# A Mamba block with routed experts: the second expert product in f16 halves, steps placed anew, and B broadcast one state at a time

## The reference

```
s = s * exp(delta * A) + delta * B * u          # per token, channel and state
y = sum over states of C * s, + u * D
...
g = sigmoid(x @ gate_w.T); the top 4 of 16, divided by their sum -> combine
h = silu(x @ e_win) * (x @ e_vin) * combine     # per expert: 256 -> 128
routed = h @ e_wout                             # 128 -> 256, summed over experts
shared = silu(x @ ws_in) * (x @ vs_in) @ ws_out # 256 -> 256 -> 256
x = x + gate * (routed + shared)
```

## Time and profile before

| | us |
|---|---|
| median of 3 runs (lowest to highest) | 2981.22 (2980.82 to 2988.78) |
| the profiled execution | 2980.19 |
| its span in the profile | 2978.4 |
| mean granted TensorE clock | 0.922 |

### The profile page before, as it was taken

One profiled execution on the slowest core, in us unless ns is written; L12 is line 12 of the kernel. 1 busy time (PEld: TensorE's weight loads), 2 busy tenths in 40 slices (PEclk: granted clock), 3 DMA queues, 4 the chain that ended last, 5 costly groups with the idle time before them and its releaser, 6 DMA issues.

```text
span 2978.4 us, 52216 instructions
## 1 busy us (share of the span) xinstructions
PE 2431.5 (82%) x16084; PEld 1908.7 (64%) x16084; DVE 2277.2 (76%) x3495; ACT 2129.4 (71%) x4033; POOL 2397.0 (80%) x2382
## 2 busy tenths in 40 slices
PE   3557988888797888979888797888979788897879
PEld 1335767667576665757667575766757666676767
DVE  4777778787787878778787877878777787877753
ACT  4786877778686777868677787767868777785641
POOL 1887898889788888888888888888978878897842
PEclk7657999999899999999999899999989999998999
DMA  1775777867676785767677677776757777676841
GB/s 67 195 172 127 167 159 164 179 135 161 147 170 157 165 177 132 163 158 162 155 156 178 138 163 158 156 171 150 167 135 169 160 165 172 135 159 140 179 102 57
DMA packets 154563, 455.99 MB, mean 153 GB/s; under 512 B 22280, under 2 KB 24968, under 8 KB 154032
## 3 DMA queue, kind: packets, MB, share of 16 engines
q0 software_dynamic: 73728, 268.47, 48.2%
q1 hardware_dynamic: 80560, 184.20, 19.9%
HBM read 166.29 MB, written 17.87 MB: 62 GB/s over the span
## 4 chain that ended last, share of the span: by engine, by line
POOL 21%; issue 20%; PE 18%; DVE 15%; ACT 14%; DMA 6%; DVEq 1%; POOLq 0%; ACTq 0%; SPq 0%
POOL db_sb L669 10%; PE bank_ps L1413 8%; DVE states L1150 5%; PE moe_ps L1431 4%; POOL y_sb L681 3%; POOL act L712 3%; DMA y_sb<-c_rows 3%; DMA th_p<-x_dram 3%; ACT c_rows L886 3%; ACT da_ps L913 3%; PE rows_ps L1349 2%; DVE bank_ps L1097 2%; POOL y_sb L690 2%; DVE act L1231 2%; DVE act L1237 1%
## 5 line engine op out<-in xcount | busy, mean ns | idle before, releaser
L669 POOL TENSOR_TENSOR db_sb<-du_sb,b_sb 128x512 f32<-128x512 f32 x1024 | 1575.2, 1710 | 80.3 <-DVE states L1150 79.8
L886 ACT ACTIVATE c_rows<-rows_ps,xd_sb 128x512 f32<-128x512 f32 x1024 | 684.8, 684 | 186.4 <-PE rows_ps L1349 93.9
L1349 PE MATMUL rows_ps<-ident,states 128*128 128x128 f32 x4096 | 646.8, 291 | 177.6 <-ACT c_rows L886 104.9
L913 ACT ACTIVATE da_ps<-delta,a_sb 128x512 f32<-128x512 f32 x1024 | 704.4, 692 | 93.2 <-DVE states L1150 91.5
L712 POOL TENSOR_TENSOR act<-act,w_sb 128x256 f32<-128x256 f32 x512 | 580.8, 1185 | 224.7 <-DMA w_sb<-w_dram 119.4
L681 POOL DMA_DIRECT2D y_sb<-c_rows x512 | 608.2, 1195 | 149.9 <-DMA y_sb<-c_rows 77.1
L1431 PE MATMUL moe_ps<-eout_sb,act 128*128 128x256 f32 x2304 | 621.5, 395 | 103.8 <-POOL act L712 101.6
L1150 DVE TENSOR_TENSOR_SCAN states<-da_ps,carry,db_sb 128x512 f32<-128x512 f32 x512 | 649.3, 1276 | 54.1 <-ACT da_ps L913 52.3
L1349 PEld LDWEIGHTS rows_ps<-ident,states 128*128 128x128 f32 x4096 | 512.6, 150 | 273.8 <-DVE states L1150 123.6
L1413 PE MATMUL bank_ps<-h2T_high,ein_w_high 128*128 128x256 f16 x2304 | 643.2, 279 | 36.0 <-DVE h2T_low L1133 15.0
L1150 DVE TENSOR_TENSOR_SCAN states<-da_ps,db_sb 128x512 f32<-128x512 f32 x512 | 617.4, 1215 | 69.2 <-ACT da_ps L913 68.3
(11 more groups left out here) (169 smaller groups left out, 2633.8 us busy)
## 6 DMA issues: line engine op xcount, KB each, us to landing
y_sb<-c_rows POOLq DMA_DIRECT2D x512, 512.0 KB, 5.5
b_sb<-b_dram SPq DMA_DIRECT2D x128, 512.0 KB, 5.1
w_sb<-w_dram SPq DMA_DIRECT2D x256, 256.0 KB, 4.4
th_p<-x_dram SPq DMA_DIRECT2D x16, 512.0 KB, 8.2
r_dram<-conv SPq DMA_DIRECT2D x16, 512.0 KB, 2.8
x<-r_dram SPq DMA_DIRECT2D x16, 512.0 KB, 5.8
out_dram<-x SPq DMA_DIRECT2D x32, 256.0 KB, 2.3
mod_p<-mod_dram SPq DMA_DIRECT2D x7, 384.0 KB, 11.2
```

What stands on the lines that cost most here:

```text
L669: pool.tensor_tensor(db_sb[:, n % NDB, :], du_sb[:, slots[t][0][0], b, :], b_sb[:, k % NBPAIR, s % BPAIR, :], ALU.mult).then_inc(sem["scal ...
L886: ac.activation(c_rows[:, n % NCR, j % CPAIR, :], rows_ps[j % 2][:, :], ACT.Copy, scale=xd_sb[:, slots[t][0][0], j, s:s + 1]).then_inc(sem ...
L913: ac.activation(da_ps[n % NDA][:, :], delta[:, slots[t][0][0], b, :], ACT.Exp, scale=a_sb[:, b, s:s + 1]).then_inc(sem["exp_done"], 1)
L1349: last = pe.transpose(rows_ps[j % 2][:, b * P:b * P + P], states[:, step % 2 * NB + b, j * P:j * P + P], ident[:, :])
```

## The change

Two things change beside the tables.

*The second expert product in f16 halves.* `eout_sb` (f32) becomes `eout_w16`, a high and a low f16 tile of the weights, lifted by 64. They are made during slot 1 in nine steps: `eo_load` (SP) brings two experts' weights into the buffers of `w_sb`, `eo_high` (ACT) writes the high part and `eo_low` (DVE) the remainder. In a unit, `e_weigh` moves ahead of `e_mul` and now needs only `e_act`. `e_mul` waits for `e_weigh` and writes its product back into the right half of the bank. Two steps are new: `e_high` (ACT) copies that half to f16 and `e_low` (DVE) writes the difference, which frees the bank. `expert_out` is six f16 matmuls. The f16 tiles have two buffers, the ring `act` keeps three. The shared units are scaled inside `e_mul`, and POOL's one-time `eout_fold` goes.

*B one state at a time.* `BPAIR, NBPAIR` go from 2, 2 to 1, 4: 256 loads of 256 KB, each of which waits until `scaled` is done with the state four before it.

All the tables have new numbers. The router's scratch tiles now lie in `zg`, so the next slot's `z_tanh` also waits for the router of the last one, and `dt_low` waits for both copies of `dt_high`.

```diff
-BPAIR, NBPAIR = 2, 2
+NACT, NACT16 = 3, 2
+BPAIR, NBPAIR = 1, 4
...
         out += [(at, ("expert_in", t, u)), (at + 0.5, ("e_tanh", t, u)), (at + 0.95, ("e_act", t, u)), (at + 1.0, ("e_mul", t, u)),
-                (at + 1.3 + TICK, ("expert_out", t, u))]
+                (at + 1.9, ("e_high", t, u)), (at + 2.2, ("e_low", t, u)), (at + 1.9 + TICK, ("expert_out", t, u))]
         if EXPERT_ORDER[u % NALL] < NE:
-            out.append((at + 1.1, ("e_weigh", t, u)))
+            out.append((at + 0.97, ("e_weigh", t, u)))
...
-SLOT = 70.6876
+SLOT = 68.7979
...
-    out += [(SLOT - 2, 0, 0, ("eout_load",)), (SLOT + 20, 0, 0, ("eout_fold",))]
+        out += [(at - 9.5, 0, 0, ("eo_load", n)), (at + 3, 0, 0, ("eo_high", n)), (at + 3.6, 0, 0, ("eo_low", n))]
...
# POOL
-                        pool.wait_ge(*bank_read(("expert_in", t, u)))
-                        place = act[:, u % 3, :]
+                        pool.wait_ge(sem["e_acted"], UNITS * nM(t) + u + 1)
+                        place = act[:, u % NACT, :]
                         pool.tensor_tensor(place, place, w_sb[:, k % NWROWS, n % WROWS, :], ALU.mult).then_inc(sem["e_weighed"], 1)
...
# ACT
-                        ac.wait_ge(sem["expert_out_done"], max(0, n - 2))
-                        ac.activation(act[:, u % 3, :], bank(key)[:, 0:HALF], ACT.Tanh, scale=0.5 / LIFT).then_inc(sem["e_tanhed"], 1)
+                        ac.wait_ge(sem["e_muled"], max(0, n - NACT + 1))
...
+                    def e_high(t, u):
+                        n = UNITS * nM(t) + u
+                        ac.wait_ge(sem["e_muled"], n + 1)
+                        ac.wait_ge(sem["expert_out_done"], max(0, n - NACT16 + 1))
+                        ac.activation(act16[0][:, u % NACT16, :], bank(("expert_in", t, u))[:, HALF:CH], ACT.Copy).then_inc(sem["e_high_done"], 1)
...
# DVE
                     def e_mul(t, u):
+                        if expert_of(u) < NE:
+                            v.wait_ge(sem["e_weighed"], routed(t, u) + 1)
+                            share = 1.0
+                        else:
+                            v.wait_ge(sem["e_acted"], UNITS * nM(t) + u + 1)
+                            share = 0.5 / LIFT ** 3
+                        place = bank(("expert_in", t, u))[:, HALF:CH]
+                        v.scalar_tensor_tensor(place, act[:, u % NACT, :], share, place, ALU.mult, ALU.mult).then_inc(sem["e_muled"], 1)
+
+                    def e_low(t, u):
                         key = ("expert_in", t, u)
-                        v.wait_ge(sem["e_acted"], UNITS * nM(t) + u + 1)
-                        place = act[:, u % 3, :]
-                        v.tensor_tensor(place, place, bank(key)[:, HALF:CH], ALU.mult).then_inc(bank_read(key)[0], 1)
+                        v.wait_ge(sem["e_high_done"], UNITS * nM(t) + u + 1)
+                        v.tensor_tensor(act16[1][:, u % NACT16, :], bank(key)[:, HALF:CH], act16[0][:, u % NACT16, :], ALU.subtract).then_inc(bank_read(key)[0], 1)
...
# PE
-                            last = pe.matmul(moe_ps[:, n, :], act[:, u % 3, n * P:n * P + P], eout_sb[:, e, :],
-                                             start=first and n == 0, stop=u % NALL == NALL - 1, skip_group_check=True)
+                            for m, (a, w) in enumerate(((0, 0), (1, 0), (0, 1))):
+                                last = pe.matmul(moe_ps[:, n, :], act16[a][:, u % NACT16, n * P:n * P + P], eout_w16[w][:, e, :],
+                                                 start=first and n == 0 and m == 0, stop=u % NALL == NALL - 1 and m == 2, skip_group_check=True)
```

125 lines of the change are left out of this document (74 added, 51 removed), and 133 rows, old and new, of the table PLACE.

## The result

| kernel | median (lowest to highest), us | ratio to before, 95% interval |
|---|---|---|
| before | 2982.01 (2976.61 to 2988.78) | 1 |
| after | 2992.6 (2984.19 to 3001.96) | 1.0031 [1.0021, 1.0042] |

The account below looks back on a forecast made before the run. No engine was taken as full: four queues in a ring, so savings count by chain share, except PE in the last stretch. Terms -7 -21 +23 +20 -9 -39 = -33 us gave 2948 us, range 2895 to 3030.

Parts of the forecast that it names:

- The weights' DMA: POOL's 119.4 us of waits for router weights: neither gained nor lost, since SP's changes at the router offset each other.
- PE, last stretch: Last chunk's final 34 units, where PE alone sets the end: 0.215 us saved per unit counts fully, -7 us.
- PE elsewhere: The other 542 units: 117 us less PE work, counted at PE's 18% chain share, -21 us.
- `e_high` and `e_low`: New steps on ACT and DVE, costed at chain shares of 14% and 15%: +23 and +20 us.
- `e_weigh` ahead: POOL weighs before e_mul, waiting for e_act 0.42 us earlier: 44 us less idle, at POOL's 21% -9 us.
- Seam: Between slots, smaller, more spread B loads let c_add's DMA land sooner: half of POOL's 77.1 us waits, -39 us.
- Setup and start: Filling slot: added loads and steps fit DVE's 39 us free, counted 0, with +10 kept and 5 either way.
- C: Rival: DVE becomes the bound through three waits per unit; up to +116 us, priced at 3020; chance 0.32.
- the deciding 26.7: Steady-slot DVE idle time in us: unless it falls below this from 35.0, the kernel is slower.
- My test for C: DVE: e_mul's waits for e_weigh plus e_low's for e_high exceed 246.5 us without e_act's waits shrinking.
- B: Rival, no difference: B's split does nothing at the seam, or clock falls to 0.90; priced 2981, chance 0.14.
- D: Rival: the new ACT and DVE steps fit into idle time, +23 and +20 become 0; 2905 us, chance 0.11.

Follow-up runs that it names:

- e13: Changed kernel with only router weights' load 6 (load 7 moves along) moved ahead of the B load and store of B on SP: 2963.49 us, ratio 0.9947.
- e5: Changed kernel with weights' loads 2, 3, 6, 9, 10 moved on SP ahead of B loads and output store: 2924.35 us, ratio 0.9815; unintended repeat 0.9799.
- e11: Kernel before with only weights' load 9 moved ahead of the output store and B load on SP: 2945.76 us, ratio 0.9870.
- e1: Kernel before with one of the second product's two matmuls left out for 16 of 18 units of each half: 2951.91 us, ratio 0.9911.
- e14: e5 with the product of the activations' low part left out in 16 of 18 units of each half: 2918.52 us, ratio 0.9797.
- e2: Kernel before with one extra unused ACT copy and one extra unused DVE difference per unit, no new hand-overs: 3031.66 us, ratio 1.0179.
- e10: e5 with both new steps cut to 16 of 256 columns and the second product fed from weights: 2877.53 us, ratio 0.9638.
- e15: e5 without the step e_low; e_high frees the bank and the product takes the high part again: 2905.13 us, ratio 0.9755.
- e16: e5 with the weighings of units 3 and 16 one place later in POOL's order: 2926.21 us, ratio 0.9827.
- e9: Kernel before with B loaded one state at a time into four buffers, at the old places: 2986.26 us, ratio 1.0014.
- e6: Changed kernel with B loaded in pairs into two buffers again, at the even states' places: 3079.75 us, ratio 1.0322.
- e8: Kernel before with the changed kernel's places for setup and slot 0 only, plus the wait of dt_low they need: 2974.51 us, ratio 0.9983.
- e3: Changed kernel with both new steps cut to 16 of 256 columns, hand-overs kept, second product fed from weights: 3001.60 us, ratio 1.0077.

## Why the prediction was wrong

The direction was wrong, and the step that failed is one sentence: "The weights' DMA (119.4 us of POOL's waits) is neither gained nor lost". I had looked at SP's new order at the seam alone. In the middle of the slot it puts a weights' load behind a B load that waits for POOL, and this costs about 25 us (e13). POOL's waits for that DMA rose from 119.4 to 150.0 us. What I had weighed at the router came out the other way: the B load and the store of r between storing the weights and loading them cost nothing there. From the store to the first load pass 1.6 to 1.9 us in all 16 chunks, where it was 3.8 in seven of them, and POOL waits 23 us less ahead of unit 2. Without load 6's stall the changed kernel stands at 0.9947, some 16 us faster than before. With weights' loads moved ahead in both, e5 stands at 0.9815 and 0.9799, and e11 at 0.9870, 16 to 21 us apart, though e11 moved one load and e5 five. So the change as such gains about half of the 33 us of my sum, and the order on SP took more than that.

Term by term:

- **PE, last stretch (-7).** The saving is there, the worth isn't. Worked out from PE's records of the last slot, the median distance from one first product to the next is 1.975 us, where it was 2.176: 0.20 a unit against my 0.215. But from unit 2 to the end the last chunk is only 2.6 us shorter. That PE alone sets the end held before (e1 took 11 us off there) and no longer holds after (e14 took off nothing).
- **PE elsewhere (-21).** Mis-sized. Work taken from PE came off at 7% in e1 and at nothing to some 11% in e14, not at 18%. By 7% the term is -8. That another engine takes PE's place on the chain at once is my reading; no run shows it.
- **`e_high` and `e_low` (+23, +20).** Right for the two together: +53 where the rule says 51 (e2), 47 to 53 where it says 43 (e10). For `e_low` alone it is too high: 18 to 19 where it says 33 (e15). `e_high` takes 383 ns and `e_low` 412, as in the rows they were read from the earlier trace rows.
- **`e_weigh` ahead (-9).** Not borne out. POOL's waits for the step before the weighing rose from 104.5 to 141.0 us, and DVE now waits 164.5 us for the weighing. No run prices it alone; in e16 two such waits were worth nothing.
- **Seam (-39).** Not priced by any run. In the trace it came as forecast and more: POOL's waits for `c_add`'s DMA fell by 38.0 us, ACT's by 75, and such a DMA lands 5.7 us after its issue at the seam (1277 to 1303 us), where it was 7.4. Against it, the same DMA now makes up 8% of the chain where it was 3%, and POOL's total idle time rose by 14 us, from 581 to 595; without the waits for the weights it fell by 17. The split alone gives nothing (e9), which the sum had said as well; what the new order gives was tested only in e6, where another wait drowns it.
- **Setup and start (0).** The start gained 10 us in the trace; in e8 it is worth 5.

Added up, the terms that runs price come to about -3 -8 +50 -5 = +34, and the changed kernel without load 6's stall measures -16. What no run prices (the seam, `e_weigh`'s move, the places of all other steps) must then have brought some 50 us. That is what I had put on the seam and `e_weigh` together, 48, but it is reached by elimination, as if the terms simply added up; the runs don't say which of the three it is. The miss of some 43 us, from -33 to +10, is in this account load 6's stall (25), PE's time (18) and the steps (some 7), less the start's 5 and some 2 of the rest.

**The rivals.** C, DVE as the bound, named the right sign and the wrong mechanism. DVE's load became 146.7 to 149.9 us, as worked out (147.3). Its idle time is 30.4 and 25.8 us in the two slots above, on both sides of the deciding 26.7 and a little above it in the mean. That was bound to agree with the result, since load and idle time add up to the slot; it doesn't say why the idle time stayed. But 125 us less on DVE change nothing (e3), and e5 is faster by 2.2% with DVE's load the same. My test for C, the two new waits above 246.5 us with `e_act`'s unchanged, came out half: 267.5 us, while `e_act`'s fell to 34.6. A hand-over's wait moves with the hand-over, so that a sum of waits judges nothing. B's clock didn't fall to 0.90: it is 0.93 and 0.95 in the two steady slots, with PE busy for 82 and 81% of them, and 0.95 and 0.93 in the same two before. Its sum was also wrong by my own numbers: with 6.6 of the 7.7 us taken back, and the last stretch kept, it is -15, 2966, not -5. B's other half, nothing gained at the seam, is shown by e9 for the split alone and by no run for the new order. D, the steps free of charge, is excluded by e2 and e10.

Two points stay open: the 39 us of loads 2, 3, 9 and 10 in the changed kernel were not taken apart further, and the bank's hold was not measured without another cost beside it.

## What to carry to other kernels

When an order is changed, walk every queue that only issues DMAs through the whole period, and for each load ask what it stands behind, what that waits for, and how long before its use it now goes out. In the two places tried (e16), a wait inside the ring of engines, POOL's for `e_act`, only moved when it was taken away. A wait for something issued late from outside came off: 109 us of it was worth 64 to 68 us. And a cut that brings nothing says little as long as such a stall stands, since the same cut was worth 47 us or more when it was gone.
